# Setup stage of a gated cross-attention kernel: vector u from columns and diagonals, biases and first tiles handled during the matrix product

## The reference, cut to what matters

```
Q = einsum('btx,dx->btd', text, Wq) + bq          # text: normalized x
K = einsum('bpx,dx->bpd', features, Wk) + bk
scores = einsum('btd,bpd->btp', Q, K) * scale
x = x + tanh(g_xattn[1]) * (softmax(scores) @ features)
```

## Time and profile before

| | us |
|---|---|
| median of three runs | 2032.49 |
| profiled execution, device time | 2033.91 |
| its span | 2032.1 |
| TensorE busy in the span | 1964.3 |
| VectorE busy | 1044.1 |
| ScalarE busy | 741.7 |
| GpSimd busy | 729.1 |
| TensorE's first matmul | 11.83 |
| first matmul of block 8 | 57.30 |
| first thin matmul of c | 98.75 |
| first transpose of the next stage | 115.15 |

### The profile page before, as it was taken

How to read it: one execution, slowest core, us unless ns; L and a number is a source line. 1 busy time by engine, 2 the same in 40 slices (tenths; PEclk the granted TensorE clock), 3 DMA queues, 4 the chain that set the end, 5 groups by cost and what they waited for, 6 DMA issues and landing times.

```text
span 2032.1 us, 37336 instructions
## 1 busy us (share of the span) xinstructions
PE 1964.3 (97%) x13968; PEld 1297.8 (64%) x13968; DVE 1044.1 (51%) x2002; ACT 741.7 (36%) x1559; POOL 729.1 (36%) x719
## 2 busy tenths in 40 slices
PE   7999999999999999999999989999999967999998
PEld 3478888885666666666665545666766745666665
DVE  5545555534555555545555654343343555555564
ACT  4411111222555555555555651111111233444442
POOL 0000000111565656555665550011010235667662
PEclk9999999999999999999999999999999988999999
DMA  6533333333222222333222453231322565666661
GB/s 209 144 99 110 100 108 103 116 102 80 65 69 66 68 64 65 77 100 72 68 64 64 121 136 103 63 94 57 83 80 59 150 198 169 200 212 203 192 213 60
DMA packets 313217, 223.86 MB, mean 110 GB/s; under 512 B 247984, under 2 KB 284848, under 8 KB 308896
## 3 DMA queue, kind: packets, MB, share of 16 engines
q1 hardware_dynamic: 286000, 209.92, 36.0%
q10 hardware_dynamic: 27120, 12.60, 2.3%
HBM read 170.76 MB, written 51.65 MB: 109 GB/s over the span
## 4 chain that ended last, share of the span: by engine, by line
PE 85%; DVE 4%; ACT 2%; DMA 2%; issue 1%; SPq 0%; POOL 0%; DVEq 0%; ACTq 0%
PE a_pr L668 12%; PE c_x_ps L1527 9%; PE b_kv_ps L1067 9%; PE b_kv_ps L1071 9%; PE d_f_ps L1947 8%; PE b_s_ps L1108 7%; PE c_t_ps L1584 7%; PE b_o_ps L1123 7%; PE d_a_ps L1734 3%; PE b_mx_ps L1083 3%; PE a_pr L664 2%; PE c_f_ps L1557 2%; PE d_s_ps L1705 2%; DVE d_y3T L1903 1%; DVE c_y2T L1476 1%
## 5 line engine op out<-in xcount | busy, mean ns | idle before, releaser
L870 POOL TENSOR_TENSOR b_probT<-b_exp,b_probT 128x448 f16<-128x448 f32 (+2 forms) x256 | 265.0, 1038 | 296.8 <-ACT b_probT L934 296.7
L448 POOL TENSOR_TENSOR cT<-ctx_raw,cT 128x375 f16<-128x375 f32 x256 | 228.2, 911 | 126.1 <-ACT cT L443 126.1
L668 PE MATMUL a_pr<-a_yT,proj_q_p 128*128 128x256 f16 x2016 | 223.2, 273 | 0.0
L668 PEld LDWEIGHTS a_pr<-a_yT,proj_q_p 128*128 128x128 f16 x2016 | 197.2, 98 | 23.5
L1071 PE MATMUL b_kv_ps<-wkv_p,cT 128*128 128x384 f16 (+1 forms) x1152 | 210.7, 326 | 0.0
L1004 DVE TENSOR_REDUCE b_nmax<-b_mx_ps 112x2 f16<-112x974 f32 x128 | 149.6, 1169 | 109.6 <-PE b_mx_ps L1083 109.5
L1067 PE MATMUL b_kv_ps<-cT,wkv_p 128*128 128x375 f16 x1152 | 199.2, 323 | 0.0
L1108 PE MATMUL b_s_ps<-b_qT,b_kT 96*128 96x448 f16 (+5 forms) x768 | 190.4, 356 | 3.2 <-DMA b_qT<-b_nrow 2.2
L1123 PE MATMUL b_o_ps<-b_probT,b_v 128*128 128x448 f16 (+5 forms) x768 | 187.3, 352 | 4.4 <-POOL b_probT L870 4.4
L932 ACT ACTIVATE b_exp<-b_s_ps 128x448 f32<-128x448 f32 (+2 forms) x256 | 137.7, 538 | 128.5 <-PE b_s_ps L1108 121.9
L1947 PE MATMUL d_f_ps<-wo_early,d_y3T 128*112 128x512 f16 x768 | 174.6, 381 | 0.0
(11 more groups left out here) (200 smaller groups left out, 2814.2 us busy)
## 6 DMA issues: line engine op xcount, KB each, us to landing
ctx_raw<-in_ctx_t SPq DMA_DIRECT2D x32, 1500.0 KB, 8.0
d_cn_raw<-in_ctx_nat SPq DMA_DIRECT2D x30, 512.0 KB
b_qT<-qk_scratch SPq DMA_DIRECT2D x32, 336.0 KB, 4.4
o_scratch<-b_o SPq DMA_DIRECT2D x128, 84.0 KB, 1.9
qk_scratch<-a_heads SPq DMA_DIRECT2D x70, 144.0 KB, 2.1
x_scratch<-c_x SPq DMA_DIRECT2D x14, 512.5 KB, 3.6
raw<-in_x SPq DMA_DIRECT2D x14, 512.0 KB, 4.0
wkv_p<-in_x SPq DMA_DIRECT2D x14, 512.0 KB, 3.3
```

What stands on the lines that cost most here:

```text
L448: pool.tensor_tensor(cT[:, p, 1, k, 0:S], ctx_raw[:, k, :], cT[:, p, 0, k, 0:S], ALU.subtract).then_inc(split_lo, 1)
L668: last = mm(pr[:, n % PR, 0:GT * P], w[:, b, k, at * P:(at + 1) * P], yT[:, g % 2, a, k, :], start=(x == 0 and k == 0), stop=(x == 2 and k ...
L870: pool.tensor_tensor(pT[0:m, c, 1, :], ex[0:m, i % 2, :], pT[0:m, c, 0, :], ALU.subtract).then_inc(p_lo, 1)
```

## The change

The vector u is computed as columns, as c is, but from wq and bk, in 128 thin matmuls that stand ahead of block 14 (`U_AT = 14`). ACT reads them and DVE adds the two parts, splits the sum into high and low, and multiplies the identity by each column of it (`diag`, 2 x 8 operations of 128 x 128). In the tail TensorE multiplies a matrix of ones by these diagonals (four matmuls of 512 columns), which puts u on all partitions. s0 becomes the product of the biases, reduced along the row by DVE and then over partitions by two matmuls of one column with ones. The bias work and the tanh move behind block 8. The x tiles get a buffer of their own, are loaded after piece 31, and are normalized behind blocks 10 and 12.

```
-                tiles_in = raw[:, 0:2, :]
+                tiles_in = sb("tiles_in", [P, 2, D], F32)
...
 # SP
                         for n, (src, _, _, runs, _) in enumerate(pieces):
+                            if n == M_PIECES + EARLY_PIECES:
+                                for t in range(2):
+                                    sp.dma_start(tiles_in[:, t, :], x[t * P:(t + 1) * P, :]).then_inc(rows_loaded[t], 16)
                             wait(sp, w_lo, n - RING + 1)
...
-                        for t in range(2):
-                            sp.wait_ge(w_lo, len(pieces) - RING + t + 1)
-                            sp.dma_start(tiles_in[:, t, :], x[t * P:(t + 1) * P, :]).then_inc(rows_loaded[t], 16)
 # ACT
-                        act.wait_ge(small_loaded, 48)
-                        act.activation(tg[:, :], gate_in[:, :], ACT.Tanh).then_inc(tanh_ready, 1)
...
+                            if i == U_AT:
+                                act.wait_ge(u_done, 1)
+                                act.activation(u_parts.rearrange("p k l -> p (k l)"), m_ps[:, 0, 0:2 * KD], ACT.Copy,
+                                               scale=1.0 / WS).then_inc(u_read, 1)
                             act.wait_ge(m_done, i + 1)
                             act.activation(Mt[:, 0, m, h * HALF:(h + 1) * HALF], m_ps[:, i % BANKS, :], ACT.Copy,
                                            scale=MS / (WS * WS)).then_inc(m_hi, 1)
+                            if i == BANKS:
+                                act.wait_ge(small_loaded, 48)
+                                act.activation(tg[:, :], gate_in[:, :], ACT.Tanh).then_inc(tanh_ready, 1)
...
 # DVE
+                        def biases():
...
+                            for i in range(2):
+                                dve.tensor_copy(b_p[:, i, 0, :], bqk_hi[:, i, :]).then_inc(bias_ready, 1)
+                                dve.tensor_copy(b_p[:, i, 1, :], bqk_lo32[:, i, :]).then_inc(bias_ready, 1)
+                            dve.tensor_tensor(both[:, :], bqk[:, 0, :], bqk[:, 1, :], ALU.mult).then_inc(multiplied, 1)
+                            dve.wait_ge(multiplied, 1)
+                            dve.tensor_reduce(col[:, KD:KD + 1], both[:, :], AX.X, ALU.add).then_inc(multiplied, 1)
+                            dve.wait_ge(tanh_ready, 1)
...
+                        def diagonals():
+                            dve.wait_ge(u_read, 1)
+                            dve.tensor_tensor(col[:, 0:KD].rearrange("p (k o) -> p k o", o=1), u_parts[:, :, 0:1],
+                                              u_parts[:, :, 1:2], ALU.add).then_inc(col_split, 1)
...
+                            for part, src in ((0, col_hi32), (1, col_lo32)):
+                                for k in range(KD):
+                                    dve.tensor_scalar(diag[:, part, k, :], ident32[:, :], src[:, k:k + 1], None,
+                                                      ALU.mult).then_inc(diag_ready, 1)
+                                dve.tensor_copy(col_p[:, part:part + 1], src[:, KD:KD + 1]).then_inc(diag_ready, 1)
...
+                            if i == BANKS:
+                                biases()
+                            if i in TILES_AT:
+                                t = TILES_AT.index(i)
+                                dve.wait_ge(rows_loaded[t], 16)
+                                norm_measure(dve, tiles_in[:, t, :], P, t)
+                                norm_scaled(dve, tiles_in[:, t, :], tiles_in[:, t, :], P, t).then_inc(y_ready, 1)
+                            if i == U_AT - 1:
+                                diagonals()
 # TensorE (columns_of holds the loops that computed c before)
                         for i in range(BANKS, 2 * KD):
+                            if i == U_AT:
+                                pe.wait_ge(bias_ready, 4)
+                                pe.wait_ge(m_lo, BANKS + 1)
+                                columns_of(wq_p, 1, 0, u_done)
...
+                        pe.wait_ge(m_lo, BANKS + 2)
+                        columns_of(wk_p, 0, 1, b_done)
+                        pe.wait_ge(diag_ready, 2 * (KD + 1))
+                        pe.wait_ge(half_ready, 2)
                         for h in range(2):
                             pe.wait_ge(m_lo, BANKS + h + 3)
-                            for n, (a, b) in enumerate(PASSES):
-                                for k in range(KD):
-                                    last = mm(m_ps[:, 2 + h, :], bk_bc[:, a, k, :], wq_p[:, b, k, h * HALF:(h + 1) * HALF],
-                                              start=(n == 0 and k == 0), stop=(n == 2 and k == KD - 1))
+                            for part in range(2):
+                                last = mm(m_ps[:, 2 + h, :], ones[:, :], diag[:, part, h * KD // 2:(h + 1) * KD // 2, :].rearrange(
+                                    "p k c -> p (k c)"), start=(part == 0), stop=(part == 1))
                             last.then_inc(b_done, 1)
                         pe.wait_ge(m_lo, BANKS + 5)
-                        for n, (a, b) in enumerate(PASSES):
-                            for k in range(KD):
-                                last = mm(m_ps[:, 4, 0:1], bk_bc[:, a, k, :], bq_p[:, b, k:k + 1],
-                                          start=(n == 0 and k == 0), stop=(n == 2 and k == KD - 1))
+                        for part in range(2):
+                            last = mm(m_ps[:, 4, 0:1], ones[:, :], col_p[:, part:part + 1], start=(part == 0), stop=(part == 1))
                         last.then_inc(b_done, 1)
```

More of the change, by code:

```diff
@@ L184, in build @@
                     bqk_hi32 = sb("bqk_hi32", [P, 2, KD], F32)
-                    bq_p = sb("bq_p", [P, 2, KD], F16)
+                    b_p = sb("b_p", [P, 2, 2, KD], F16)
                     c_parts = sb("c_parts", [P, KD, 2], F32)
-                    ones = sb("ones", [P, P], F32)
-                    bk_bc = sb("bk_bc", [P, 2, KD, P], F16)
+                    u_parts = sb("u_parts", [P, KD, 2], F32)
+                    col = sb("col", [P, KD + 1], F32)
+                    col_hi = sb("col_hi", [P, KD + 1], F16)
+                    col_hi32 = sb("col_hi32", [P, KD + 1], F32)
+                    col_lo32 = sb("col_lo32", [P, KD + 1], F32)
+                    col_p = sb("col_p", [P, 2], F16)
+                    both = sb("both", [P, KD], F32)
+                    ones = sb("ones", [P, P], F16)
+                    diag = sb("diag", [P, 2, KD, P], F16)
                     BANKS = 8
@@ L308, in _ @@
                         act.wait_ge(b_done, 1)
-                        act.activation(c_parts.rearrange("p k l -> p (k l)"), m_ps[:, 0, 0:2 * KD], ACT.Copy,
+                        act.activation(c_parts.rearrange("p k l -> p (k l)"), m_ps[:, 1, 0:2 * KD], ACT.Copy,
                                        scale=1.0 / WS).then_inc(b_read, 1)
@@ L312, in _ @@
                             act.wait_ge(b_done, h + 2)
-                            act.activation(u_bc[:, h * HALF:(h + 1) * HALF], m_ps[:, 2 + h, :], ACT.Copy,
-                                           scale=1.0 / WS).then_inc(b_read, 1)
+                            act.activation(u_bc[:, h * HALF:(h + 1) * HALF], m_ps[:, 2 + h, :], ACT.Copy).then_inc(b_read, 1)
                         act.wait_ge(b_done, 4)
@@ L330, in _ @@
                             low(n)
[L331 to L340, removed]
-                            for k in range(KD):
-                                dve.tensor_scalar(bk_bc[:, part, k, :], ones[:, :], src[:, 1, k:k + 1], None,
-                                                  ALU.mult).then_inc(bias_ready, 1)
@@ new lines, in diagonals @@
+                        def diagonals():
+                            dve.wait_ge(u_read, 1)
+                            dve.tensor_tensor(col[:, 0:KD].rearrange("p (k o) -> p k o", o=1), u_parts[:, :, 0:1],
+                                              u_parts[:, :, 1:2], ALU.add).then_inc(col_split, 1)
+                            dve.wait_ge(col_split, 1)
+                            dve.wait_ge(multiplied, 2)
+                            dve.tensor_copy(col_hi[:, :], col[:, :]).then_inc(col_split, 1)
+                            dve.wait_ge(col_split, 2)
+                            dve.tensor_copy(col_hi32[:, :], col_hi[:, :]).then_inc(col_split, 1)
+                            dve.tensor_tensor(col_lo32[:, :], col[:, :], col_hi[:, :], ALU.subtract).then_inc(col_split, 1)
+                            dve.wait_ge(col_split, 4)
+                            dve.wait_ge(ident_ready, 1)
+                            for part, src in ((0, col_hi32), (1, col_lo32)):
[3 more added lines that the diff above has]
+                                dve.tensor_copy(col_p[:, part:part + 1], src[:, KD:KD + 1]).then_inc(diag_ready, 1)
@@ L387, in _, with columns_of @@
                                     last.then_inc(m_done, 1)
+                        def columns_of(weights, bias, bank, done):
```

(13 more changed lines are left out.)

25 lines of the change are left out of this document (11 added, 14 removed).

## The result

The changed kernel takes 2025.13 us (median of six runs, 2023.39 to 2025.57) against 2032.51 for six runs of the kernel before: ratio 0.9961, 95% interval 0.9949 to 0.9974. That is 7.4 us faster, 0.36%. I had forecast 2023.9 in a range of 2020.2 to 2028.2. Two later sets put it at 0.9949 (0.9936 to 0.9963) and 0.9952 (0.9938 to 0.9965), 10.3 and 9.5 us, so the forecast of 8.6 lies between the three.

What follows compares the result with a forecast made beforehand. TensorE, busy 97% of the span, was taken to bound the kernel. -2.46 - 1.66 + 3.32 + 1.5 - 10.2 + 0.9 = -8.6 gave 2025.3 us profiled, 2023.9 as median; range 2020.2 to 2028.2 with rivals 1 to 4.

Steps and rivals of the forecast that it cites:

- Start: TensorE's first matmul, at 11.83 before: with tanh moved on ACT, weight copies go sooner and it starts at 9.37, -2.46.
- Wait for bank 0: TensorE's 1.66 wait for the first `Mt` piece goes as DVE's bias work no longer leaves the buffer ring: -1.66.
- x tiles and DVE's work: Tile loads after piece 31 and DVE's added work in the second half fit in free time: cost 0.
- The clock behind it: Product 14, behind u's thin stretch, pays a fall of the granted clock: +1.5, bounds 0 and 1.7.
- Tail: End of c to first transpose, 13.08 before: 2.9 at 1.2 GHz, -10.2 taken; 2.15 at 2.4 GHz, -10.95.
- First transposes: Tile 0's eight transposes run at the low clock, 1.97 instead of 1.08: +0.9, upper bound 0.9 + 1.5.
- Everything behind the setup: Stages after the first transpose keep instructions and relative waits; the effect is that instant's shift, plus the clock found next.
- the ring that gives the hole back: Rival 1, buffer ring of early weight pieces: TensorE still waits 1.66 for `Mt`; -6.9, 2025.6; 12%.
- the start that brings nothing: Rival 4, start of TensorE's stream: tanh's place brings nothing; -6.1, 2026.4; 5%.
- the slower case: Rival 5: clock stays at 1.2 GHz from u's thin stretch through products 14, 15 and tail into projections; 2037; 3%.
- The case without any fall: Rival 2: clock doesn't fall behind the thin stretches, no 1.5, no 0.9, tail -10.95; -11.8, 2020.7; 18%.
- The low clock into the projections: Rival 3: low clock goes on through tail, transposes and first projections; -7.1 to -5.6, 2026.1 in the middle; 15%.

Runs made afterwards that it cites:

- u alone: Kernel before with only u as columns, diagonals and the new tail, which also drops the 16 spreading operations: 2032.76 us against 2033.66, ratio 0.9999.
- the tiles put back: Changed kernel with x tiles back in the ring's buffers, loaded after the last piece and normalized last: 2029.81 us, ratio 0.998 to the kernel before.
- the held-back pieces: Changed kernel with SP issuing weight pieces 2 and 3 only after 0 and 1 landed, run twice: 2023.37 and 2022.53 us.
- the doubled stretch: Changed kernel with u's 128 thin matmuls run twice before block 14: 2028.79 us, ratio 0.9979 to the kernel before.
- the tiles alone: Kernel before with only the x tiles in their own buffer, loaded after piece 31, normalized behind blocks 10 and 12: 2034.79 us, ratio 1.0008.

## Why the prediction was right, point by point

**Start, -2.46 forecast.** 11.83 to 9.42, and 2.46 with the tanh alone. The landings read from the trace carried over: ACT's copies began within 0.1 of where I put them. The clock's rise, for which I allowed 0.85 either way, came 5.4 after the first matmul here (4.5 before), which costs half a us.

**Wait for bank 0, -1.66.** Gone. The last early copy ended at 50.49 where I had 49.8, and the first `Mt` copy started at 50.40. The experiments hold both halves: with the hole left it stays, with the biases moved it goes. I gave the whole credit to the move, though. The change also drops the 16 spreading operations, and in "u alone" that by itself had block 8 start 2.2 earlier and left 0.31 of the wait.

**x tiles and DVE's work, 0.** Right in the sum, incomplete in the reason. I looked at who waits for piece 32 and not at piece 31, right ahead of the tiles; alone the edit costs 0.8 there. And I booked the tiles' move at zero and the tail at -10.2, without saying that the second needs the first: DVE ended normalizing at 111.5, and with TensorE's tail ending sooner that would have been next. The question "what is late next" belonged at the tail.

**Thin stretch, +3.32.** 3.30.

**The clock behind it, +1.5.** The step that missed in the profiled execution: 0. It is 1.7 where it comes, and it came in one of three profiles of the changed kernel, and in those of u alone, of the tiles put back and the first of the two with the held-back pieces. Of seven profiles with a single thin stretch for u and no extra dense work, four paid. On that count the term would have been some 1.0 on average (an estimate, 4/7 of 1.7); no single execution shows such a value. My bounds held it. That it can fall without an idle gap stands as I read it from the earlier trace rows: besides the doubled stretch, in six of the thirteen profiles the fall lies inside c's stretch, as at 101.65 in the kernel before. Why it comes in one execution and not in another is open. The Trainium skill ("TensorE: Matmul & The Clock Gate", section "Why this matters for your kernels") speaks of idle gaps alone. The fall behind 4.01 of waiting, with the tiles alone, agrees with it; those inside the thin stretches don't.

**Tail, -10.2.** 2.08 from the end of c to the first transpose, against 2.9 forecast at the low clock and 2.15 at the full one. So -11.0 in this profile, since the clock fell only at 103.6, behind TensorE's part of it; the third has 2.87, and there the clock fell at 101.9. ACT ends it, as forecast.

**First transposes, +0.9.** 107.99 - 103.67 = 4.32 against 3.44 before: +0.9. The clock then rose while only transposes had run (the rows at 104 and 106, then 107.2), so the upper bound did not come. The clearest case is the profile of the tiles put back, where TensorE was idle from 103.8 to 111.76, then ran transposes alone, and the clock was back at 114.5, before anything else ran:

```profile
104.00:111.70 7.70, 0.00 (x0) 0.00 (x0) 4.90 (x13) 0.42 (x2) 1.11 (x2) 0.50 0.06 24
...
112.00:114.40 2.40, 2.40 (x13) 2.40 (x13) 0.00 (x0) 0.66 (x1) 0.00 (x0) 0.50 0.47 133
```

It isn't always so early: with u alone the 3.6 of transposes passed at 0.50 and the rise came at 120.4, 1.7 into the projections, and in the second profile of the held-back pieces it came at 107.4, again 1.7 into them. The Trainium skill (same page, "Part 4: PE-mode transpose") says that transposes don't count as busy; these, of float32, brought the clock back in the profiles where nothing else ran before the rise.

**Everything behind the setup, 0.** This is the other miss, a term that I put at nothing. By terms the first projection is 10.6 earlier, and the span only 8.9 shorter. Across the thirteen profiles of this case the time from the start of the first projection to that of the last matmul is 1905.3 to 1909.7, for the same instructions: 1908.0 in the profile of before, 1909.7, 1909.3 and 1909.6 in the three of the changed kernel. The fall at 2005 is 1.5 of the 1.7 between before and after. It is also in the third profile (2006.5), not in the second. That one has another fall at 1181.7, and one at 478.6 that lasts 6.8 where the other two have 3.4. Across the profiles these falls stand at a few fixed distances from the first projection or are missing: 371 to 373 in nine of thirteen, 1074 in two, 1896 to 1897 in three. The three shortest times, 1905.3 to 1906.5, are among the four without the first of these. So the spread of this part is, in the main, falls that come or don't. Whether the changed kernel's offset makes them likelier or three profiles are too few, I can't say; that is open. I had named a later stage that changes by more than a us as a sign of being wrong, and it is one: two errors of opposite sign, 2.0 of gain too little up to the projections (1.5 and 0.8, less some 0.4 ahead of block 14, where the later rise of the clock took its half us) and 1.7 lost behind them, made the sum closer than its parts. That the profiled execution took 2025.33, where I had 2025.3, is luck to that extent; the start, the wait, the thin stretch and the first transposes are not.

The rivals: the ring that gives the hole back, the start that brings nothing and the slower case did not come. The case without any fall came in part. The low clock into the projections did not come in the three profiles; it did in the second of the held-back pieces, where the first 48 projection matmuls took 8.80 instead of 7.97, and with u alone.

## What to carry to other kernels

Price a cut in a tail by the engine that ends it next: u's matmuls (10 us of TensorE) brought nothing until DVE's normalization was moved, and that move brought nothing until they were cut; in a sum of separate edits both would be wrong. An engine that works its instructions in order and leaves a ring of buffers for 3.8 us is missed by whoever sits behind the ring, even 15 us later. A change that moves work and also drops some should be tried both ways. And when a cut is worth 0.4%, read it at a landmark of the trace (first transpose, first projection) as well as in the median: the rest of the program varied by 4 us.

## What the runs showed of the hardware

The granted clock can fall in a stretch of matmuls of one or two columns, 45 to the us at 2.4 GHz, with TensorE 1.00 busy: at 88.5, within the doubled stretch, and at 101.65 in the kernel before. It doesn't always: four of seven profiles have a fall within 1.3 behind u's single stretch, and twelve of thirteen within or up to 2.0 behind c's. With the second stretch replaced by dense matmuls of the same length there was no fall (one profile). Eight float32 transposes took 0.9 more at 1.2 GHz (1.97 against 1.08); with the tiles put back the clock was at 2.4 GHz again after 2.7 of nothing but transposes, with u alone it wasn't after 3.6 of them. Four 512 KB loads issued together landed the first one 5.8 after its issue; with two together ACT had it 4.5 after.
